# An attention loop whose value matmuls follow one step behind instead of two, with all output projections moved into the next head

## The reference

```python
Q = (nx @ Wq.T).reshape(B, S, H, dk).transpose(0, 2, 1, 3)     # B = 2, S = 2048, H = 4, dk = 64
Kc = nx @ Wkc.T
Vc = nx @ Wvc.T
scores = jnp.einsum('bhsd,btd->bhst', Q, Kc) * scale
attn = jax.nn.softmax(scores, axis=-1)
out = jnp.einsum('bhst,btd->bhsd', attn, Vc)
X = X + out.transpose(0, 2, 1, 3).reshape(B, S, d) @ Wo.T
nx = _rmsnorm(X, g2)
...                                                            # router, top 2 of 8 experts, shared expert
```

## Time and profile before

| | us |
|---|---|
| median of three runs | 1449.37 |
| lowest and highest | 1449.15, 1457.35 |
| the profiled execution | 1457.35, span 1455.5 |
| loop, first scores to last copy of O | 235.1 to 1115.4 |

### The profile page before, as it was taken

How to read it: one execution, slowest core, us unless ns; L and a number is a source line. 1 busy time by engine, 2 the same in 40 slices (tenths; PEclk the granted TensorE clock), 3 DMA queues, 4 the chain that set the end, 5 groups by cost and what they waited for, 6 DMA issues and landing times.

```text
span 1455.5 us, 19322 instructions
## 1 busy us (share of the span) xinstructions
PE 1312.1 (90%) x6008; PEld 928.4 (64%) x6008; DVE 1071.3 (74%) x2143; ACT 892.1 (61%) x1450; POOL 381.5 (26%) x282
## 2 busy tenths in 40 slices
PE   4777677999999999999999999999997899999995
PEld 2334544665666666676675666666664798888774
DVE  4957877887887776777886777786874767546678
ACT  2355563766767757666688666666575856555452
POOL 0443341112211122211112311111155001623346
PEclk9989786999999999999999999999997999999998
DMA  5000015300000000000000001000012233655645
GB/s 196 1 1 29 30 58 183 106 1 1 1 0 1 1 1 1 0 1 1 1 1 1 1 1 44 1 1 1 22 44 73 90 100 113 205 148 158 184 127 156
DMA packets 56418, 75.82 MB, mean 52 GB/s; under 512 B 8383, under 2 KB 48063, under 8 KB 56064
## 3 DMA queue, kind: packets, MB, share of 16 engines
q1 hardware_dynamic: 36030, 46.29, 9.8%
q0 software_dynamic: 6144, 16.79, 3.7%
q10 hardware_dynamic: 14146, 11.52, 2.4%
HBM read 37.27 MB, written 37.22 MB: 51 GB/s over the span
## 4 chain that ended last, share of the span: by engine, by line
PE 64%; DVE 18%; ACT 6%; issue 5%; POOL 4%; DMA 2%; ACTq 1%; POOLq 0%; SPq 0%; DVEq 0%
PE PS L1804 8%; PE PS L1751 6%; PE PS L1702 6%; PE PS L1734 6%; PE PS L1753 6%; PE PS L1737 6%; PE PS L1752 6%; DVE mx L1161 5%; PE PS L1830 4%; DVE PL L1191 4%; PE PS L1715 3%; POOL y L1536 2%; PE PS L1688 2%; PE PS L1788 1%; POOL xbuf L1524 1%
## 5 line engine op out<-in xcount | busy, mean ns | idle before, releaser
L1161 DVE TENSOR_REDUCE mx<-PS 128x1 f32<-128x512 f32 x512 | 344.6, 686 | 112.6 <-PE PS L1702 111.3
L770 ACT ACTIVATE PT<-PS 128x1024 f32<-128x1024 f32 x256 | 262.6, 1026 | 233.5 <-PE PS L1737 222.6
L1516 POOL TENSOR_TENSOR PL<-PT,PH 128x1024 fp32r<-128x1024 f32 x61 | 145.6, 2387 | 560.0 <-ACT PH L775 414.3
L775 ACT ACTIVATE PH<-PT 128x1024 fp32r<-128x1024 f32 x256 | 271.3, 1060 | 8.1
L1191 DVE TENSOR_TENSOR PL<-PT,PH 128x1024 fp32r<-128x1024 f32 x195 | 238.6, 1223 | 42.3 <-ACT PH L775 40.8
L1751 PE MATMUL PS<-PH,VH 128*65 128x512 f32 x512 | 221.8, 433 | 8.9 <-DVE PL L1191 6.7
L1753 PE MATMUL PS<-PL,VH 128*65 128x512 f32 x512 | 203.7, 398 | 0.0
L1752 PE MATMUL PS<-PH,VL 128*65 128x512 f32 x512 | 203.2, 397 | 0.0
L1702 PE MATMUL PS<-KA,Q 128*128 128x512 f32 x384 | 164.1, 440 | 21.9 <-DVE mx L1161 15.4
L1734 PE MATMUL PS<-Q,KA 128*128 128x512 f32 x384 | 129.0, 417 | 2.5 <-POOL KB L1493 2.5
L1737 PE MATMUL PS<-Q,KB 65*128 65x512 f32 x384 | 122.8, 402 | 0.0
(11 more groups left out here) (239 smaller groups left out, 2484.0 us busy)
## 6 DMA issues: line engine op xcount, KB each, us to landing
xbuf<-xT SPq DMA_DIRECT2D x26, 384.0 KB, 4.4
xg<-xbuf SPq DMA_DIRECT2D x78, 128.0 KB
ybuf<-yo ACTq DMA_DIRECT2D x78, 128.0 KB
nxT<-in_wexp SPq DMA_DIRECT2D x9, 768.0 KB, 4.4
x<-in_x SPq DMA_DIRECT2D x8, 512.0 KB, 11.6
x_scratch<-x SPq DMA_DIRECT2D x2, 2048.0 KB, 7.2
nxT<-x_scratch SPq DMA_DIRECT2D x32, 128.0 KB
out<-X SPq DMA_DIRECT2D x32, 128.0 KB, 2.3
```

The lines of the kernel that those rows point to most:

```text
L770: act.activation(PT[:, gs % 2, :], PS[:, bk:bk + 2, :].rearrange("p a n -> p (a n)"), ACT.Exp, scale=0.125).then_inc(sem("pt"), 1)
L775: act.activation(PH[:, gs % 4, :], PT[:, gs % 2, :], ACT.Copy).then_inc(sem("pt_h"), 1)
L1161: dve.tensor_reduce(mx[:, half, i, c:c + 1], PS[:, k, :], AX, ALU.max).then_inc(sem("dve_out"), 1)
L1516: pool.tensor_tensor(PL[:, gs % 3, :], PT[:, gs % 2, :], phf[:, gs % 4, :], ALU.subtract).then_inc(sem("pl_g"), 1)
```

## The change

`av` and `o_out` of step `gs - 1` are now run in step `gs` (before: `gs - 2`), and after the loop one step is left over instead of two. `PH` has three buffers instead of four and is written once `av(gs-3)` is done. `O` holds both blocks of a head (2048 queries). The 16 projections of a head all stand in the next head: eight from unit 4 to 49, eight from 50 to 92; in head 4 from 4 to 30 and 31 to 60. The projections of head 7 all stand in the tail, each ahead of its norm.

```diff
-def proj_jobs(bh, qc):
-    return [("proj", bh, 8 * qc + i) for i in range(8)]
+def proj_jobs(bh):
+    return [("proj", bh, i) for i in range(NT)]
...
-        todo += spread(proj_jobs(bh, 0), 56, 94)
         if bh > 0:
-            todo += spread(proj_jobs(bh - 1, 1), 8, 46)
+            m, e = (30, 60) if bh == 4 else (49, 92)
+            todo += spread(proj_jobs(bh - 1)[:8], 4, m) + spread(proj_jobs(bh - 1)[8:], m + 1, e)
...
     norm = norm_jobs(1)
-    last = [x for j, p in enumerate(proj_jobs(7, 1)) for x in (norm[j], p)] + norm[8:]
+    last = [x for j, p in enumerate(proj_jobs(7)) for x in (p, norm[j])] + [norm[NT]]
...
-    PH = sb("PH", [P, 4, 1024], F32R, c=c3)
+    PH = sb("PH", [P, 3, 1024], F32R, c=c3)
     PL = sb("PL", [P, 3, 1024], F32R, c=c3)
-    O = sb("O", [65, 1024], c=c3)
+    O = sb("O", [65, S], c=c3)
...
             w.wait_ge(sem("pt"), gs + 1)
-            if gs >= 4:
-                w.wait_ge(sem("av"), 2 * (gs - 3))
-            act.activation(PH[:, gs % 4, :], PT[:, gs % 2, :], ACT.Copy).then_inc(sem("pt_h"), 1)
+            if gs >= 3:
+                w.wait_ge(sem("av"), 2 * (gs - 2))
+            act.activation(PH[:, gs % 3, :], PT[:, gs % 2, :], ACT.Copy).then_inc(sem("pt_h"), 1)
...
             w.wait_ge(sem("av"), 2 * gs + n + 1)
-            if qc:
-                pe_of(w, ("proj", bh, 7, 0))
-            elif bh:
-                pe_of(w, ("proj", bh - 1, 15, 0))
-            act.activation(O[:, n * 512:n * 512 + 512], PS[0:65, 4 + n, :], ACT.Copy).then_inc(sem("o"), 1)
+            if bh:
+                pe_of(w, ("proj", bh - 1, 8 * qc + 7, 0))
+            act.activation(O[:, q0:q0 + 512], PS[0:65, 4 + n, :], ACT.Copy).then_inc(sem("o"), 1)
...
-                if part and gs >= 2:
-                    av(gs - 2, part - 1)
+                if part and gs >= 1:
+                    av(gs - 1, part - 1)
                 run(work, LOOP[gs, part])
-        for gs in range(NGS - 2, NGS):
-            av(gs, 0)
-            av(gs, 1)
+        av(NGS - 1, 0)
+        av(NGS - 1, 1)
```

More of the change, by code:

```diff
@@ L781, in o_out @@
                 return
+            q0 = qc * 1024 + n * 512
             w.wait_ge(sem("av"), 2 * gs + n + 1)
-            if qc:
-                pe_of(w, ("proj", bh, 7, 0))
-            elif bh:
-                pe_of(w, ("proj", bh - 1, 15, 0))
-            act.activation(O[:, n * 512:n * 512 + 512], PS[0:65, 4 + n, :], ACT.Copy).then_inc(sem("o"), 1)
+            if bh:
+                pe_of(w, ("proj", bh - 1, 8 * qc + 7, 0))
+            act.activation(O[:, q0:q0 + 512], PS[0:65, 4 + n, :], ACT.Copy).then_inc(sem("o"), 1)
         def norm(b, i):
@@ L912, in _ @@
                     exp(gs + 1)
-                if part and gs >= 2:
-                    o_out(gs - 2, part - 1)
+                if part and gs >= 1:
+                    o_out(gs - 1, part - 1)
                 run(work, LOOP[gs, part])
-        for gs in range(NGS - 2, NGS):
-            o_out(gs, 0)
-            o_out(gs, 1)
+        o_out(NGS - 1, 0)
+        o_out(NGS - 1, 1)
         for s in range(-2, NTL + 2):
@@ L1190, in low @@
                 w.wait_ge(sem("av"), 2 * (gs - 2))
-            dve.tensor_tensor(PL[:, gs % 3, :], PT[:, gs % 2, :], phf[:, gs % 4, :], ALU.subtract).then_inc(sem("pl_v"), 1)
+            dve.tensor_tensor(PL[:, gs % 3, :], PT[:, gs % 2, :], phf[:, gs % 3, :], ALU.subtract).then_inc(sem("pl_v"), 1)
         def norm_root(b):
@@ L1515, in low @@
             after_last("pl_g")
-            pool.tensor_tensor(PL[:, gs % 3, :], PT[:, gs % 2, :], phf[:, gs % 4, :], ALU.subtract).then_inc(sem("pl_g"), 1)
+            pool.tensor_tensor(PL[:, gs % 3, :], PT[:, gs % 2, :], phf[:, gs % 3, :], ALU.subtract).then_inc(sem("pl_g"), 1)
         def scatter(b, i):
@@ L1714, in proj @@
             k = bank("proj", bh, i, 0)
-            pe.matmul(PS[:, k, 0:257], O[0:65, n * P:n * P + P], woa[0:65, bh % 4, :], start=True,
+            pe.matmul(PS[:, k, 0:257], O[0:65, i * P:i * P + P], woa[0:65, bh % 4, :], start=True,
                       stop=True).then_inc(sem("pe_use"), 1)
@@ L1744, in av @@
             qc, kc = divmod(i, 16)
-            h, r, t, c = gs % 4, gs % 3, b * NT + kc, slice(n * 512, n * 512 + 512)
+            r, t, c = gs % 3, b * NT + kc, slice(n * 512, n * 512 + 512)
             w.wait_ge(sem("pt_h"), gs + 1)
@@ L1750, in av @@
                 w.wait_ge(sem("o"), 4 * bh + 2 * qc + n - 1)
-            pe.matmul(PS[0:65, 4 + n, :], VH[:, t, :], PH[:, h, c], start=(kc == 0), stop=False)
-            pe.matmul(PS[0:65, 4 + n, :], VL[:, t, :], PH[:, h, c], start=False, stop=False)
+            pe.matmul(PS[0:65, 4 + n, :], VH[:, t, :], PH[:, r, c], start=(kc == 0), stop=False)
+            pe.matmul(PS[0:65, 4 + n, :], VL[:, t, :], PH[:, r, c], start=False, stop=False)
             pe.matmul(PS[0:65, 4 + n, :], VH[:, t, :], PL[:, r, c], start=False, stop=(kc == 15)).then_inc(sem("av"), 1)
```

## The result

| | us |
|---|---|
| before, median of 10 runs | 1453.52 (1449.15 to 1458.36) |
| changed, median of 10 runs | 1461.94 (1455.52 to 1466.69) |
| changed / before | 1.0052, 95% interval 1.003 to 1.0076 |
| profiled execution of the changed kernel | 1461.01, span 1459.0 |

The change costs about 7.6 us by the ratio (its interval is 4.4 to 11 us; the two medians differ by 8.4). I had forecast no difference (-0.3 us). The time lies in the class that I thought likeliest, within 1%, and at the upper edge of the range, but the sign is clear: it is slower. The forecast of 1449.1 us also stood on a median of three runs, 1449.37; over ten runs the kernel before has 1453.52, so 4.2 of the 12.8 us between forecast and result are the base and not the change.

The account below looks back on a forecast made before the run. TensorE was taken to bound the attention loop, POOL-paced scatters the end of head 7. Terms -3.5 + 1.2 - 1.5 + 0 + 3.5 = -0.3 us gave 1449.1 us against the 1449.37 median; range 1440 to 1462.

Parts of the forecast that it names:

- the class that I thought likeliest: Whole kernel: time the same as before within 1% (14.5 us), chance 0.86.
- No stall for the low parts: 246 steps up to step 23 of head 7: value matmuls never wait for PL, smallest slack 0.27 us; 0 us.
- The last eight steps: End of head 7: TensorE waits for PL almost every step, but VectorE's scatters set the pace; 0 us.
- The start: Loop start: six value matmuls (2.6 us) move into step 1, 1.4 us hidden in waits; +1.2 us, ends 0 and +2.6.
- Head 7 by the earlier copies of O: Second step of head 7: weight split starts 0.5 us earlier and the clock may stay up; -1.5 us, ends 0 and -5.
- The clock part: Head 7: 7 us at the lower clock cost 3.5; three tenths of that counted as chance of no fall.
- Head 0: Head 0 loses its eight projections of 0.44 us each, as TensorE bounds it; -3.5 us, ends 0 and 6.8.
- The tail: Tail start: eight more projections, 7.8 us in sum, partly offset by work during the root wait; +3.5 us, ends +2 and +8.
- the third rival: Tail pays the full 7.8 us and stays at the lower clock, 3.5 us more; 1457 us, chance 0.15.
- The head start behind the root: Tail: root moves to step 1, so TensorE can do about 2 us of the next tile's work while it waits.
- Placement: Heads 1 to 7: 16 projections each at nearly the same units, TensorE's sum unchanged; 0 us, bounds -3 and +3.
- the prediction's own signs of being wrong: PL waits in all heads; heads 1 to 6 changed over 1 us each; second 1.2 GHz tail stretch; scatter start unmoved.

Follow-up runs that it names:

- e1: Kernel before with only the value matmuls and copies of O moved to one step behind instead of two; ratio to before 1.0002.
- e9: e1 with the second block's projections at units 4 to 49 (4 to 46 in head 4) instead of 8 to 46; ratio to before 1.0023.
- e7: Changed kernel with value matmuls and copies of O two steps behind again, three PH buffers kept; 1527.6 us, ratio to before 1.0511.
- e4: Changed kernel with the low parts of step 3 of heads 1, 3 and 5 on VectorE instead of POOL; ratio to before 1.0022.
- e3: Changed kernel with projections back at units 8 to 46 and 56 to 94, except in head 4; ratio to before 1.0038.
- e5: Changed kernel with eight tail projections moved to units 62 to 95 of head 7, head 6's 16 at units 4 to 60 there; ratio to before 1.0096.
- e6: Kernel before with the low parts of step 3 of heads 1, 3 and 5 on VectorE instead of POOL; ratio to before 0.9999.
- e8: Changed kernel, units of before in heads 1 and 3, no POOL low part in head 5's step 3, eight tail projections moved into head 7; 1444.91 us, ratio 0.9938.

## Why the prediction was wrong

By its own steps, against the second profile of before:

- *No stall for the low parts, 0 us.* Right. e1 shows it alone, and the waits of line 1749 in the changed kernel show none ahead of the scatters. Reading the slack between `PL(g-1)` and the slot of step g was enough.
- *The last eight steps, 0 us.* Right: 8.6 us of waits for `PL`, little more than the 6.7 of before, and the scatter stretch took 41.5 us against 42.4.
- *The start, +1.2.* Wrong by its size: head 0 takes 96.1 us in e1 and 96.2 in before. The value matmuls that moved into step 1 cost nothing that can be seen.
- *Head 7 by the earlier copies of O, -1.5.* The number came near (-2.3) by luck, the reason was wrong: e1 has the earlier copies and no gain, e9 has the projection at unit 4 and all of it. The clock part was a matter of the execution.
- *Head 0, -3.5.* Right: 96.1 in e1, 92.3 in the changed kernel, -3.8.
- *The tail, +3.5 and not the +7.8 of its projections' sum.* Right. The executions with eight projections in the tail took 68.8 to 70.7 us for the first 20 tiles (mean of seven 69.8), those with 16 took 72.7, 73.9, 74.2 and, in e7, 75.1 (mean 74.0): +4.2. The clock was not held down, as the third rival had it: 0.95 over these tiles in the changed kernel, 0.90 and 0.93 before. The head start behind the root, which the prediction walked through, is there: in the changed kernel TensorE idled 1.50 us for tile 5 instead of the 3.44 us of the earlier trace rows. TensorE in the changed kernel:

```profile
1139.66 0.41 PE L1786 MATMUL PS<-ident,xg 128*128 128x128 f32 x2 [1.50 <-DVE xl L1369]
```

- *Placement, 0 with bounds of 3.* This is the step that failed. Heads 1, 3 and 5 lost 2.1 + 3.8 + 3.5 = 9.4 us and head 4 1.9; a change of more than 1 us in these heads was among the prediction's own signs of being wrong. I treated placement as a matter of TensorE's sum and of how densely jobs stand, and asked of each move only whether somebody waits. Nobody waits for POOL here by a semaphore. An instruction of VectorE lasts four times as long because POOL is at work beside it. The shorter lag, which the sum also has at 0, brought POOL's low part up to the query low part (e1), and the first projection at unit 4 instead of 8 put the query low part behind its start (e9). e4 takes the meetings away for 5.9 us in these heads: about 0.85 each for the wait, and 1.7 twice for the lower clock behind it. e9 makes them with one edit on e1, and its three heads grow by 8.2. Of the 3.5 that e4 leaves, e3 shows the units to matter in heads 1 and 3 beyond the meeting (114.6 and 117.6 in e4, 112.9 and 115.9 in e3); which jobs collide there was not followed further. The 1.9 us of head 4 come with the 16 projections ahead of unit 60: 101.2 in e1, 103.1 to 103.4 in all that pack them so at the shorter lag.

The sum as measured: -3.9 (head 0) + 9.4 (heads 1, 3, 5) + 1.9 (head 4) - 0.7 (head 2) - 2.3 (head 7) - 0.9 (scatters) + 4.2 (tail) = +7.7, against 0.52% of 1453.5 = 7.6. That they meet within 0.1 is luck: one profiled execution stands for each term of the loop, and the interval of the ratio spans 4.4 to 11 us.

One sum of the prediction was also off: the lower ends of its terms add up to 12.8 us below the forecast and not to 15, since the tail's lower end is +2. The range did not hang on it.

The trace of before had signs of it, one in the very stretch of the tightest slack. Timeline of VectorE in before:

```profile
1059.55 2.36 DVE L1301 TENSOR_TENSOR_SCAN r_e<-r_e 128x8 f32<-128x8 f32 x1
...
1063.34 0.17 DVE L1306 TENSOR_TENSOR_SCAN r_e<-r_e 128x8 f32<-128x8 f32 x1
```

A scan of eight elements takes 0.17 us, and 2.36 beside POOL's low part, which ran from 1059.49 to 1061.89. I read only the slack. Another is in head 1: a scaling of `nx` (line 1135) took 1.86 us at 391.85 instead of 0.34, beside POOL's low part of 391.17 to 393.56.

Of the rivals, none named this. The nearest was the tail at full price; the tail was not the cause of the miss.

## What to carry to other kernels

When a change moves work in time, list the pairs of VectorE and POOL instructions that can now overlap, not only the waits. In this kernel VectorE's tensor-tensor, tensor-scalar and scan instructions on SBUF stood while POOL computed a low part. Which of the two starts first decides who pays, so a shift of a fraction of a microsecond can turn a harmless overlap into a costly one, and on an engine that others wait for the price can include a stretch at the lower clock. A cheap way to find them is to compare the longest with the median duration of each group, in the trace of before and of after; a rise of VectorE's busy time at an equal count says at once that they are there. Work that has to go somewhere belongs in a stretch that another engine bounds: 15 projections fitted into the scatter stretch for nothing, while five more in front of it cost 7 us.

## What the runs showed of the hardware

- VectorE's query low part (two SBUF inputs, 64x512) takes 0.69 us and, begun 0.28 us after POOL's tensor operation of 2.5 us, 2.77: it ends 0.55 us after POOL's end. Three in the changed kernel, three in e5, three in e9, none in e1, e3, e4, e6, e7 or e8.
- Begun 0.23 us before POOL's low part, the same instruction keeps its 0.69 us, and POOL's takes 2.71 instead of 2.38 (e1, head 1).
- Two SBUF tensors are not needed. A tensor-scalar of `X` by a column of scalars, 128x256, took 1.86 us instead of 0.34 in before and 2.50 in e1; one of 1x39 took 1.74 instead of 0.17 at 1070.55 in before. In the changed kernel 90 row maxima and 20 of the multiply-adds into `X2`, which have an input in PSUM, began beside a low part of POOL and stayed at 0.69 and 0.49 us at most.
- An instruction of POOL need not be long to do it: VectorE's low part of 1.22 us took 1.44 us at 336.30, begun 0.25 us after POOL's copy of 64x512 (0.61 us). POOL's next copy of the same size, begun 0.51 us after VectorE's, took 1.40.
- One waiting time of TensorE, 1.90 us and 1.91 us, was followed by the lower clock in one execution of the same kernel and not in the other. In the changed kernel the wait of 2.01 us in head 1 was not followed by it (1.00 over the next 10 us), that of 2.00 in head 3 was (0.83).
